# Experts in tiles of 256 rows, low parts moved between VectorE and GpSimd, results scattered by token

## What is computed

```python
def _L0_ffn_ref(x, router_w, gate_w, gate_b, up_w, up_b, down_w, down_b):
    D_MODEL, D_FF, N_EXPERTS, TOP_K = (256, 512, 8, 2)
    xf = x.reshape(b * s, d)
    probs = jax.nn.softmax(xf @ router_w.T, axis=-1)
    topv, topi = jax.lax.top_k(probs, TOP_K)
    mask = jnp.zeros_like(probs).at[jnp.arange(n)[:, None], topi].set(1.0)
    probs = probs * mask
    probs = probs / (probs.sum(axis=-1, keepdims=True) + 1e-09)
    g = jnp.einsum('nd,edf->nef', xf, gate_w) + gate_b
    u = jnp.einsum('nd,edf->nef', xf, up_w) + up_b
    h = jax.nn.silu(g) * u
    expert_out = jnp.einsum('nef,efd->ned', h, down_w) + down_b
    y = jnp.einsum('ne,ned->nd', probs, expert_out)
x = _layernorm(x + _L0_ffn_ref(...), axis=-1)
```

## Time and profile before

| | |
|---|---|
| time, median of 3 runs | 1888.91 us (1878.64 to 1890.14) |
| profiled execution | 1898.8 us, span of the core 1897.0 us |
| PE busy | 1631.2 us, 86% of the span |
| DVE / ACT / POOL busy | 1049.1 / 924.4 / 784.5 us |
| mean granted TensorE clock | 0.895 of full speed |

### The profile page before, as it was taken

One profiled execution on the slowest core, in us unless ns is written; L12 is line 12 of the kernel. 1 busy time (PEld: TensorE's weight loads), 2 busy tenths in 40 slices (PEclk: granted clock), 3 DMA queues, 4 the chain that ended last, 5 costly groups with the idle time before them and its releaser, 6 DMA issues. The chain is left out here.

```text
span 1897.0 us, 34831 instructions
## 1 busy us (share of the span) xinstructions
PE 1631.2 (86%) x11631; PEld 1442.4 (76%) x11631; DVE 1049.1 (55%) x2308; ACT 924.4 (49%) x1786; POOL 784.5 (41%) x798
## 2 busy tenths in 40 slices
PE   4999999999999999679999999992499999999600
PEld 3899898989898999567777777781388888888500
DVE  3455455555555555446676676665644554544346
ACT  4566566656665666424344344340154544544245
POOL 6444444444444444211221121110356666666264
PEclk9999999999999999878888888885599999999855
DMA  3000000000000000110111111100335445545144
GB/s 106 7 18 19 18 18 18 18 18 18 18 18 18 18 18 13 41 43 31 45 44 38 45 31 45 51 28 12 128 117 161 151 153 161 161 144 137 49 121 123
DMA packets 96766, 114.90 MB, mean 61 GB/s; under 512 B 18306, under 2 KB 77082, under 8 KB 96666
## 3 DMA queue, kind: packets, MB, share of 16 engines
q1 hardware_dynamic: 89178, 93.01, 15.4%
q0 software_dynamic: 7488, 20.46, 4.2%
HBM read 84.50 MB, written 24.64 MB: 58 GB/s over the span
## 5 line engine op out<-in xcount | busy, mean ns | idle before, releaser
L253 POOL TENSOR_SCALAR_AFFINE_SELECT a_decay<-a_decay 128x256 f32<-128x256 f32 x256 | 113.5, 447 | 375.3 <-ACT a_decay L327 374.5
L435 DVE TENSOR_TENSOR a_probs<-a_ps_s,a_decay 128x384 f32<-128x384 f32 x256 | 131.7, 553 | 186.2 <-PE a_ps_o L615 171.5
L875 POOL TENSOR_TENSOR b_probs<-b_probs,b_top 128x1232 f32<-128x1232 f32 x32 | 73.3, 2290 | 344.1 <-DVE b_top L1000 344.1
L265 POOL TENSOR_TENSOR a_qk_lo<-a_qk,a_qk_hi 128x512 fp32r<-128x512 f32 x128 | 164.5, 1285 | 23.9 <-POOL a_qk_hi L262 23.9
L290 ACT ACTIVATE a_qk_exp<-a_ps_qk 128x512 f32<-128x512 f32 x128 | 76.6, 598 | 190.3 <-PE a_ps_qk L528 180.3
L528 PE MATMUL a_ps_qk<-a_xT_hi,a_w_hi 128*128 128x256 f32 x512 | 146.7, 286 | 4.7 <-ACT a_qk_relu L291 4.7
L528 PE MATMUL a_ps_qk<-a_xT_lo,a_w_hi 128*128 128x256 f32 x512 | 145.4, 284 | 0.0
L528 PE MATMUL a_ps_qk<-a_xT_hi,a_w_lo 128*128 128x256 f32 x512 | 145.1, 283 | 0.0
L1179 PEld LDWEIGHTS b_ps_o<-b_v,b_pT 77*128 77x128 f32 x1024 | 136.0, 207 | 0.0
L1179 PE MATMUL b_ps_o<-b_v,b_pT 77*128 77x16 f32 x1024 | 134.2, 266 | 0.0
L325 ACT ACTIVATE a_decay<-a_ps_c,a_c_now 128x256 f32<-128x256 f32 x256 | 124.1, 485 | 11.0 <-PE a_ps_c L593 10.2
(11 more groups left out here) (277 smaller groups left out, 5307.8 us busy)
## 6 DMA issues: line engine op xcount, KB each, us to landing
e_gu_raw<-in_L_ffn_gate_w SPq DMA_DIRECT2D x23, 512.0 KB, 4.1
e_gu_raw<-in_L_ffn_up_w SPq DMA_DIRECT2D x23, 512.0 KB, 5.3
e_dn_raw<-in_L_ffn_down_w SPq DMA_DIRECT2D x23, 512.0 KB, 6.7
y_sorted<-e_y_out SPq DMA_DIRECT2D x23, 512.0 KB, 2.8
a_x_in<-in_x SPq DMA_DIRECT2D x16, 256.0 KB, 2.7
a_x_res<-in_x SPq DMA_DIRECT2D x16, 256.0 KB, 2.7
x_rows<-a_x SPq DMA_DIRECT2D x16, 256.0 KB, 2.3
b_x_in<-x_rows SPq DMA_DIRECT2D x16, 256.0 KB, 2.8
```

Source lines behind the costliest of these rows:

```text
L253: pool.affine_select(out=d, in_=d, compare_op=ALU.is_ge, fill=0.0, base=0, pattern=[[0, 2], [1, P]], channel_multiplier=-1)\
L265: pool.tensor_tensor(qk_lo[g][:], qk[:], qk_hi[g][:].bitcast(F32), ALU.subtract).then_inc(qk_lo_done, 1)
L435: vec.tensor_tensor(probs[h][:], ps_s[h][:, 0:TRI], decay[h][:], ALU.mult)\
```

## The change

- T becomes 256. The list has (8192 − 8)//256 + 8 = 39 tiles, 9,984 rows. A tile loads the same 1.5 MB of weights.
- A chunk's gate and up results (256 columns each) share a bank, and each of the four chunks has its own bank, `gate` and `hid`; `hid_hi`, `hid_lo` and the result's bank are double by tile.
- `hid_low` goes from VectorE to GpSimd. The low parts of the weights go from GpSimd to VectorE: the gate and up ones in 4 pieces of 128x512 (`gu_low`), the down ones in one of 128x1024 (`dn_low`). `gu_high` becomes two instructions and stands behind the first silu.
- The store by slot goes. GpSimd scatters each tile's rows by token and choice into `y_rows` with 2 indirect DMAs (`scatter_rows`), between `hid_low` of chunks 0, 1 and the gathers.
- The inversion makes the column matrices of a batch in 2 instructions rather than 8, sums the two choices apart, and works out where each row's result goes (`goal`); slots that no token has go to rows of their own behind the others.
- `combine` loads its rows with 16 plain DMAs, all issued at its start, in groups of 4 blocks with a buffer for each. ScalarE weighs the first row and normalises, GpSimd adds x2, VectorE adds the second row and takes the statistics. The table of ln and exp is loaded once. Nothing is a loop.

```diff
-        self.T = 512
+        self.T = 256
...
             def tile(t, par, turn):
                 if has(t, 2):
-                    sp.wait_ge(gu_lo_done[par], turn + 1)
+                    e_next, e = experts(t, 1, 2, t + 2)
+                    sp.wait_ge(gu_lo_done[par], LOW_PARTS * (turn + 1))
                     sp.wait_ge(dn_lo_done[par], turn + 1)
-                    e_next, e = experts(t, 1, 2, t + 2)
                     load_weights(e, par)
...
-                if has(t, -1):
-                    store(t - 1, 1 - par)
                 if has(t, 1):
-                    load_biases(e_next, 1 - par)
+                    if has(t, -1):
+                        sp.wait_ge(hid_done[FC - 1], t)
+                    load_bias(e_next, 1 - par)
+                    if has(t, -1):
+                        sp.wait_ge(y_kept, t)
+                    load_dn_bias(e_next, 1 - par)
...
+            def scatter_rows(t, par, turn):
+                pool.wait_ge(target_ready[par], turn + 1)
+                pool.wait_ge(y_kept, t + 1)
...
+                for blk in range(TB):
+                    pool.indirect_dma_start(y_rows, bass.IndirectOffsetOnAxis(target[par][:, blk:blk + 1], 0),
+                                            y_out[par][:, blk, :], None).then_inc(y_stored[par], 16)
...
             def tile(t, par, turn):
-                if has(t, 1):
-                    low_parts(1 - par, turn + par)
...
+                hid_low(0)
+                hid_low(1)
+                if has(t, -1):
+                    scatter_rows(t - 1, 1 - par, turn - 1 + par)
                 if has(t, 2):
                     gather_rows(par, turn + 1)
+                hid_low(2)
+                hid_low(3)
...
+            def gu_low(par, turn, part):
+                k, half = part // 2, part % 2
+                cols = slice(half * FF, (half + 1) * FF)
+                vec.wait_ge(gu_hi_done[par], KC * turn + k + 1)
+                vec.tensor_tensor(gu_lo[par][:, k, cols], gu_raw[par][:, k, cols], gu_hi[par][:, k, cols].bitcast(F32),
+                                  ALU.subtract).then_inc(gu_lo_done[par], 1)
...
             def down(t, par, turn):
                 pe.wait_ge(dn_lo_done[par], turn + 1)
-                for n in range(2):
-                    pe.wait_ge(hid_lo_done[n], (t + 1) * (FC // 2))
+                for f in range(FC):
+                    pe.wait_ge(hid_lo_done[f], t + 1)
...
+        @block.sync
+        def _(sp):
+            for i in range(GROUPS):
+                for k in range(2):
+                    sp.dma_start(y[i][k][:], y_blocks[k][:, i * G:(i + 1) * G, :]).then_inc(loaded[i], 16)
...
-                        pool.indirect_dma_start(y[par][k][:, j, :], None, y_sorted,
-                                                bass.IndirectOffsetOnAxis(slots[k][:, n:n + 1], 0))\
-                            .then_inc(gathered[par], 16)
+                    n = i * G + j
+                    pool.wait_ge(weighed, n + 1)
+                    pool.tensor_tensor(resid[i][:, j, :], y[i][0][:, j, :], x2_all[:, n, :], ALU.add).then_inc(first_added, 1)
```

More of the change, by code:

```diff
@@ new lines, in _ @@
+            vec.tensor_copy(first[:], ps_token[0]).then_inc(token_step, 1)
+            vec.tensor_copy(second[:], ps_token[1]).then_inc(token_step, 1)
+            vec.wait_ge(token_step, 2)
+            vec.tensor_tensor(held[:], first[:], second[:], ALU.add).then_inc(token_step, 1)
+            vec.tensor_scalar(second[:], second[:], 1.0, float(plan.TOKENS), ALU.is_ge, ALU.mult).then_inc(token_step, 1)
+            vec.wait_ge(token_step, 4)
+            vec.tensor_scalar(token[:], held[:], 1.0, 0.0, ALU.subtract, ALU.max).then_inc(token_step, 1)
@@ L1743, in _ @@
+            for part in range(LOW_PARTS):
+                gu_low(0, 0, part)
+            dn_low(0, 0)
             x_low(0, 0)
@@ L1804, in _, with combine @@
             down(TILES - 1, (TILES - 1) % 2, (TILES - 1) // 2)
[L1807 removed]
+def combine(nc, sh, plan, x2_all, gates, y_rows, out):
     D, NBK = sh.D, plan.BLOCKS
[L1810 removed]
+    G = 4
     GROUPS = NBK // G
[L1812 removed]
     with ExitStack() as ctx:
@@ L1917, in decoder_layer @@
+            weigh_first(0)
+            weigh_first(1)
+            for i in range(GROUPS):
+                root(i)
+                if i + 2 < GROUPS:
+                    weigh_first(i + 2)
+                if i:
+                    normalise(i - 1)
+            normalise(GROUPS - 1)
 def decoder_layer(nc, x, ctx_1024, mask, Wq, Wk, Wv, Wo, Wa, ba, xWq, xbq, xWk, xbk, xWv, xbv, xWo, xbo,
```

368 lines of the change are left out of this document (178 added, 190 removed).

## The result

The changed kernel takes 1939.0 us (median of 4 runs, 1934.5 to 1940.6), against 1889.5 us for the kernel before on the same chip (1878.6 to 1891.1). The ratio is 1.027, with a 95% interval of 1.023 to 1.030. So it is **slower**, and 1939 lies above the range of the prediction, 1807 to 1913. The profiled execution took 1934.5 us with a span of 1932.5. That is 35.5 us more than the 1897.0 of before.

What follows compares the result with a forecast made beforehand. PE bounded the old tiles; the prediction took a ring through GpSimd to bound the new ones at 11.7 us. Preparation −13.6, tiles +43 and combine −52 sum to −22.6 us: 1888.9 becomes 1866 us, range 1807 to 1913.

Steps and rivals of the forecast that it cites:

- Preparation, −13.6 us: Experts' preparation before the first gate matmul: shorter by 13.6 us, bounds 8 and 16.
- Combine, −52 us: Final combine stage: 54 us in place of 106.4, bounds on the saving 60 and 38.
- The ring: Tiles: keep_y, GpSimd's DMAs and hid_low, then down; 10.4 us between down products, 11.7 with holds and clock.
- 0.17 later, scatters tile t−1: Ring link after keep_y: GpSimd starts its scatters 0.17 us later; with the gathers the DMAs take 4.85 us.
- The handovers on either side of `down`: Ring links around down: 0.1 us wait for chunk 3's low part before, 0.2 us to keep_y after.
- the two holds: VectorE and GpSimd in a tile: dn_low against scatters 0.4 us, gu_low pieces against hidden low parts 0.5 us.
- The clock: PE's pause ahead of down lowers its clock: 0 to 2.3 us a tile, 0.4 taken.
- Rival 2: Tiles: pause ahead of down drops the clock every tile; full price gives 13.6 us a tile, 1940 us; chance 0.23.
- Rival 1: Tiles: the ring is short or PE stays the bound, 9.0 to 11.1 us a tile; chance 0.27.
- rival 3: Combine stays near 80 us as engines take turns and loads and stores share DMA engines; 1892 us; chance 0.10.
- That the weights do not bind: Tiles: weight loads do not set the time, at 190 GB/s for 2.2 MB in 11.7 us.
- The signs: Changed profile if right: clock below 1.00, PE 80 to 85% busy, largest wait ahead of down, combine 47 to 62 us.

Runs made afterwards that it cites:

- e3: Changed kernel with 18 more matmuls of 256 columns, their result overwritten, ahead of each down product: 1897.6 us, 1.006 of the kernel before.
- e4: Changed kernel with gu_low and dn_low subtracting only one column per piece in the loop's tiles: 1877.2 us, 0.995 of the kernel before.
- e5: Changed kernel with the gathers ahead of the scatters and tile_index at the top of VectorE's tile: 1887.1 us, 0.999 of the kernel before.
- e10: Changed kernel with hid_low on VectorE, gathers and tile_index early, and weight pieces, roundings and silus spread: 1801.9 us, 0.953 of the kernel before.
- e11: Changed kernel with a one-column memset on GpSimd between the wait for keep_y and the first scatter: 1939.4 us (one run).

## Why the prediction was wrong, point by point

**Preparation, −13.6 us: right.** The first gate matmul was predicted near 1358.6 and stands at 1358.59. That it fits to the hundredth is luck, but the parts fit too: the first gather starts 9.8 us earlier (9.3 predicted), from it to the transposes it is 1.9 us less (2.5 predicted) and from there to the gate matmul 1.9 us less (1.8 predicted).

**Combine, −52 us: right, a little small.** It takes 48.4 us; 54 was predicted, with 7 us for holds between GpSimd and VectorE and bounds of 47 and 68. The holds are there: VectorE's 32 additions take 642 ns in the mean, where 487 was read from the earlier trace rows, 5 us in all. With them VectorE's 8 groups take 33 us, where 35 and 7 were put. In front of them stand 7.7 us and behind them 7.8, where 6 and 6 were put.

**The ring: right in every link, mis-sized at its first DMA.** By the step "0.17 later, scatters tile t−1": it is 0.82. I took the distance at which a subtraction starts. That is 0.65 us a tile, 25 us in all. The trace of the kernel before had the right row, and I read past it: the gather at 1361.04 of the earlier trace rows ends a wait for `e_index`, and the casts that make it end at 1360.13, which is 0.91 us earlier.

```profile
1359.89 0.24 DVE L1693 CAST e_index<-e_token 128x4 uint32<-128x4 f32 x2
```

The four DMAs take 5.05 us (4.85 and 0.4 of hold predicted), hid_low of chunks 2 and 3 1.90 (1.5 and 0.5). The handovers on either side of `down` take 0.51, where 0.3 was taken. Together the two holds were sized a little too high, by 0.3 us.

**The clock: wrong, and the main term.** The failed step is "slow gate and up products also eat the pause, and PE has room outside `down`; of 0 to 2.3 us I take 0.4". The full price of 2.3 was for a down product wholly at the lower level. The measured one is 4.47 − 2.88 = 1.6 us, since the clock stayed down for 15 to 17 of the 24 matmuls. That is 1.2 more than taken, 46 us in 39 tiles. The stretches around 1506 us show why: the clock falls as `down` begins and is back before it ends, so it hits exactly the part of PE's work that lies **in** the ring. The slack of PE lies in the gate and up products, which run at 1.00 and can't use it up. That the clock would fall was read rightly from the earlier trace rows; that most of its price would be absorbed had no row behind it. e3 shows the cause directly, e4 and e5 within one kernel each.

**The balance.** 0.65 for the start of the scatter, 1.19 for the clock, 0.21 for the handovers and −0.27 for the holds are 1.78 us, the 13.47 − 11.7. With the last, shorter tiles it makes 525.5 − 461 = 64.5 us. `combine` gave 5.6 back. That is 58.9 us in the profiled executions (as 35.7 − (−22.6) = 58.3), and the rest of the 73 us is the spread between profiled runs and medians: the profile of before was 10 us above its median, that of after 5 us below.

**The rivals.** Rival 2 with its full clock price, p = 13.6 and 1940 us, is what happened in kind. That its number is within 1 us is luck: it has 2.3 us for the clock, where 1.6 was measured, and nothing for the start of the scatter, which took 0.65. Its chance of 0.23 was too low: its "against" (half of what the clock takes is taken from idling) was an argument without a row. Rival 1 and rival 3 fell. That the weights do not bind held, up to 234 GB/s in e10.

**The signs.** Clock below 1.00, PE's largest wait ahead of `down` with chunk 3's low part as releaser, GpSimd without a gap from the scatter to it, pieces of `gu_low` above 0.69 us: all as listed. PE's busy share was 79%, just under the 80 to 85 expected. One sign of being wrong showed as well: the scatters' mean was 1169 ns from 1400 to 1700 us, and not 960.

## What to carry to other kernels

Sum the ring from one use of a result to the next, not only each engine's total, and ask of each link in it whether it needs to be there: here two scatters whose results are wanted only much later cost 102 us until they stood last in the queue. If a ring leaves TensorE a pause in each turn, find out which work follows the pause, and price that work at the lower clock in full if it is itself in the ring. Before you move a DMA ahead of a wait, check what its index waits for, and before you move a subtraction, what the other engine does at the new place. Put something short between a wait and an indirect DMA if there is something to put: by e11 and e5 the DMA's start runs on beside it. No run here gains time by this.
